# TensorE runs six products into an unread PSUM bank ahead of each look-up of maxima in the attention layer

## What is computed

```python
z = h @ W.T
s_src = z @ w1
s_dst = z @ w2
e = leaky_relu(s_src[src] + s_dst[dst], negative_slope=0.01)
m = segment_max(e, dst, num_segments=n)
num = exp(e - m[dst])
den = segment_sum(num, dst, num_segments=n)
alpha = num / den[dst]
w_e = (rel_alpha * alpha)[:, None]
h_agg = segment_sum(w_e * z[src], dst, num_segments=n)
return h_agg + bias_w
```

## Time and profile before

| | |
|---|---|
| time, median of 3 runs | 9725.82 us (9722.43 to 9730.15) |
| time of the profiled execution | 9727.96 us |
| its span from the first to the last instruction | 9726.4 us |
| attention stage, by the trace | 3338 to 5345 us |
| looks in it | 244 (196 groups, 48 of them with two blocks) |
| granted TensorE clock, mean over the span | 0.872 |

### The profile page before, as it was taken

One profiled execution on the slowest core, in us unless ns is written; L12 is line 12 of the kernel. 1 busy time (PEld: TensorE's weight loads), 2 busy tenths in 40 slices (PEclk: granted clock), 3 DMA queues, 4 the chain that ended last, 5 costly groups with the idle time before them and its releaser, 6 DMA issues. The chain is left out here.

```text
span 9726.4 us, 155325 instructions
## 1 busy us (share of the span) xinstructions
PE 7678.1 (79%) x38400; PEld 4799.3 (49%) x38401; DVE 4294.4 (44%) x10706; ACT 3170.9 (33%) x5260; POOL 5560.6 (57%) x5296
## 2 busy tenths in 40 slices
PE   1698888888888566666665799999999888888886
PEld 0354444444444355555554344444444656666654
DVE  6887777774443466666666210000000323323323
ACT  0012334565555466655554000000000232333232
POOL 4788888887775000000000577777775477777775
PEclk6899999999999766656666899999999999999998
DMA  3223445566666433333222899999999322222222
GB/s 111 73 89 119 143 163 171 201 219 228 212 219 210 148 131 114 112 101 98 94 87 73 292 333 337 345 334 340 324 356 332 117 78 77 77 78 77 77 78 66
DMA packets 563180, 1661.59 MB, mean 171 GB/s; under 512 B 115314, under 2 KB 312030, under 8 KB 519495
## 3 DMA queue, kind: packets, MB, share of 16 engines
q1 hardware_dynamic: 324442, 1129.76, 33.2%
q0 software_dynamic: 206976, 473.99, 16.1%
q10 hardware_dynamic: 31536, 54.94, 1.6%
HBM read 1174.46 MB, written 483.82 MB: 170 GB/s over the span
## 5 line engine op out<-in xcount | busy, mean ns | idle before, releaser
L909 PE MATMUL wide<-ring 128*128 128x392 bf16 x14112 | 2499.8, 339 | 501.7 <-DVE ring L839 262.6
L529 POOL DMA_INDIRECT z_got<-z_table,z_idx x1568 | 2131.9, 1360 | 596.8 <-issue 429.2
L909 PEld LDWEIGHTS wide<-ring 128*128 128x128 bf16 x14112 | 1408.0, 100 | 1593.3 <-issue 821.8
L1578 POOL DMA_INDIRECT l_rows<-h_table,l_recs x1568 | 1564.3, 998 | 626.9 <-issue 477.8
L1487 POOL DMA_INDIRECT sorted_recs<-dn_rec_in,type_f x1568 | 1526.6, 974 | 647.7 <-issue 471.7
L1029 POOL DMA_DIRECT2D rows<-z_edges x196 | 103.9, 530 | 2086.5 <-PE wide L362 1876.8
L1390 PE MATMUL wide<-stream,X 128*128 128x512 f32 (+1 forms) x2548 | 1044.8, 570 | 63.1 <-DMA stream<-c_dense 59.0
L373 PE MATMUL wide<-rows,onehot 128*128 128x130 f32 x3904 | 888.1, 417 | 232.2 <-DVE A L390 232.2
L373 PEld LDWEIGHTS wide<-rows,onehot 128*128 128x128 f32 x3904 | 820.9, 319 | 293.0 <-DVE A L390 291.3
L373 PE MATMUL wide<-l_rows,l_onehot 128*128 128x128 f32 x3904 | 584.0, 311 | 361.9 <-DVE X L391 361.8
L1677 DVE TENSOR_TENSOR l_rows<-l_filters,l_rows 128x1024 f32<-128x1024 f32 x196 | 240.3, 1226 | 1334.3 <-DMA l_rows<-h_table,l_recs 1316.6
(11 more groups left out here) (255 smaller groups left out, 8427.8 us busy)
## 6 DMA issues: line engine op xcount, KB each, us to landing
stream<-w_dense SPq DMA_DIRECT2D x252, 1792.0 KB
stream<-c_dense SPq DMA_DIRECT2D x84, 1792.0 KB
z_edges<-z_got POOLq DMA_DIRECT2D x196, 528.0 KB
rows<-z_edges POOLq DMA_DIRECT2D x196, 528.0 KB, 3.8
dst_bc<-in_dst_row SPq DMA_DIRECT2D x196, 512.0 KB, 3.6
c_dense<-A SPq DMA_DIRECT2D x49, 1568.0 KB
w_dense<-A SPq DMA_DIRECT2D x49, 1568.0 KB
c_dense<-H SPq DMA_DIRECT2D x49, 1568.0 KB
```

The lines of the kernel that those rows point to most:

```text
L529: e.indirect_dma_start(out=z_got[:, s, t, :], out_offset=None, in_=z_table, in_offset=bass.IndirectOffsetOnAxis(ap=z_idx[:, s, t:t + 1], a ...
L909: ins = e.matmul(banks[:, bass.ds(to[v], 1), int(m > 0), 0:WC].rearrange("p a x -> p (a x)"), lhsT=slots[:, k, m * P:(m + 1) * P], rhs=slo ...
L1578: e.indirect_dma_start(out=rows[:, k, t, :], out_offset=None, in_=h_table, in_offset=bass.IndirectOffsetOnAxis(ap=recs[:, k, t, R_DST:R_DS ...
```

## The change

In the loop over the blocks of a group, before the waits for `s_ot` and `s_q`, TensorE now issues 6 products of 512 bf16 columns, with the unit matrix as the stationary operand and the unit matrix repeated four times as the moving one. They write bank 6, which nothing reads, and they wait for nothing and signal nothing. They are called "the fill" below. With 244 looks these are 1464 products. No other instruction is removed, added or moved.

```diff
+FILL = 6
...
                         e.matmul(look, lhsT=zero_h[0:1, :], rhs=zero_h[0:1, 0:6 * TILES], start=True, stop=False)
                         with e.Fori(lo, hi):
                             e.reg_add(c, c, 1)
+                            for _ in range(FILL):
+                                e.matmul(bank[6][:, 0:4 * P], lhsT=ident_h[:, :],
+                                         rhs=ident_h[:, :].unsqueeze(1).to_broadcast([P, 4, P]), start=True, stop=True)
                             e.wait_ge(s_ot, c)
                             e.wait_ge(s_q, c)
                             e.sem_inc(note["pe"], 1)
```

## The result

| | before | after |
|---|---|---|
| median, us | 9724.12 (4 runs) | 9786.75 (4 runs) |
| ratio | | 1.0066, 95% interval 1.0054 to 1.0078 |
| first look to last look, from the trace | 1991 us | 2051 us |

The changed kernel is slower by 63 us, 0.66%. The forecast was 9732 us; the time is inside the range, but on the slower side of it, not within 0.2% of before. The products of the looks start between 3340.7 and 5392.0 us of the span after, against 3338.4 and 5329.6 us before: the whole loss is in the stage of attention.

What follows compares the result with a forecast made beforehand. VectorE was taken to set the pace of attention's one-block groups. Lost 79 us and gained 73 us, net +6 us on 9725.8 us, gave 9732 us; range 9692 to 9795 us for 8 in 10.

Steps and rivals of the forecast that it cites:

- What bounds the stage: In attention, VectorE sets the pace of one-block groups; TensorE's speed counts only in two-block groups, with waits of 65.5 and 70.2 us.
- The fill's own time: Ahead of the look, six products take 2.5 us at 1.2 GHz, or 1.3 at 2.4 GHz, 1.4 with hand-over.
- Second looks: Ahead of the 48 second looks TensorE is idle 4.43 us, so the fill is hidden at either clock: cost 0.
- The price of a late look: First looks behind sums at 1.2 GHz come 1.0 us late, 2.3 if the fill is slow too; the stage grows in full.
- The gain for one pair of blocks: In two-block groups, first-block sums at 2.4 GHz save 1.7 us each, 82 us over all 48.
- How often the clock is up: In attention, 65 of 196 groups are cold at their sums; 43 of 48 two-block sums run fast.
- The sum of +6 us: Whole kernel: 79 us lost to late looks against 73 us gained in two-block groups, net +6 us.
- the slower rival: Clock falls in the 3.42 us between look and sums in 120 groups: net +92 us, 9818 us; chance 0.30.
- the wash: Whole kernel within 19 us of no change, 9707 to 9745 us; chance 0.46.
- The faster one: Attention's clock stays up, falling only behind the 48 second looks: net -34 us, 9692 us; chance 0.22.
- the one with no effect on the clock: Attention's clock stays at 0.62 and every first look is late: +390 us, 10118 us; chance 0.02.
- The page's rule: Clock falls in waits between matmul bursts, so the stretch between look and sums costs at nearly every group: +92 us.

Runs made afterwards that it cites:

- six, two and four: The changed kernel (six products ahead of each look) plus two while TensorE waits for ScalarE and four ahead of the sums; stage 1978 us, ratio to before 0.9979.
- two and four, full rows: Kernel before, plus two products while TensorE waits for ScalarE, four ahead of the sums, and spreading widened to 128 rows; stage 1927 us, ratio 0.9931.

## Why the prediction was right or wrong

- **What bounds the stage.** Right. Behind fast sums nothing got faster in a group of one block, and the gain is only in groups of two.
- **The fill's own time.** Right: 1.46 us for six at 2.4 GHz in the timeline, where 1.3 and a hand-over were forecast.
- **Second looks.** Right: none is late.
- **The price of a late look.** Right: 104.7 us over 103 looks is 1.02 us, forecast 1.0 and a few at 2.3; single looks are 0.1 to 2.1 us late. The delay did add to the stage in full.
- **The gain for one pair of blocks.** Right: 5.18 to 3.58 us is 1.6, forecast 1.7.
- **How often the clock is up.** This is the step that failed, and the prediction had called it open. It took 65 groups as cold at their sums: the 48 behind a second look, and 17 more. The clock was down at the start of the sums behind 95 of 195 last looks, those 48 and 47 more, and in 31 groups of one block it was still up there but fell during the sums. So 103 looks were late and not 65. It took 43 of the 48 first blocks of a pair as fast; 23 ran wholly at 2.4 GHz, 13 in part and 12 not at all, and the two waits that were to fall to some 60 us came to 93.7. So the loss was 104 us and not 79, the gain 42 us and not 73. Both errors have one cause, that the clock falls behind the look more often than in a third of the groups, and they add up to 56 us, about the distance from the forecast to the result. The windows show it, and two experiments confirm it, one by filling the light stretch (73 us back) and one by filling the rows of the products that it already has (56 us back).
- **What was overlooked in that step.** The spreading was counted as 1.7 us of products in the light stretch together with the look. The trace gives their busy time, not how much of the array they use. Made full, beside the fill, they let the clock fall ahead of the sums in 37 of 169 cases and not in 69.
- **The range.** The time is inside it, but the outcome that was given the best chance, within 19 us of before, did not come. The sum of +6 us was a small difference of two terms that were both wrong; the range held because it reached to most of the slower rival.
- **The rivals.** The result lies between the wash and the slower rival, by the slower one's mechanism: 103 late looks, where it was said to decide from about 85 cold groups on. The faster one and the one with no effect on the clock fell. The page's rule (the Trainium skill, "TensorE: Matmul & The Clock Gate", "HAM oscillation — how this bites in real kernels") stood nearer to the result than the sum did: +92 us was taken by it, +6 by the sum, and +63 was measured. It speaks of waits between bursts of matmuls, though, and the trace agrees with it only in part: the stretch that cost the clock in the windows from 3941 to 3944 holds light work, TensorE being busy 0.48, 0.38 and 0.16 of each microsecond.

## What to carry to other kernels

In this kernel a fill that was to keep TensorE's clock up paid only in the stretch in which the clock is lost, not in the gap that was easiest to reach. So read in 1 us windows where the clock rises and where it falls, and fill ahead of the fall. Look at the slack of that place at the lower clock, since the fill takes twice as long (0.43 against 0.22 us a product) just where the clock was lost. Before products are added, see how many rows the existing ones use: widening them with zeros gained 56 us of the stage beside the fill and 20 us beside the one in the light stretch, but nothing without a fill, where the stage was 5 us longer.

## What was not expected of the hardware

- Six products with 32 rows left the granted clock at 0.58 where six with 128 rows, of the same count and columns, and as long at the same clock, brought it to 0.82. Eight spreading products made full changed it from 0.82 to 0.88 beside a fill and from 0.62 to 0.64 without one.
- Without a fill the full rows did not hold the clock: it was up at the end of 104 of 195 last looks and at the start of 19 of the sums behind them.
- Three products ahead of each look cost as much as six: 2052 and 2051 us for the stage.
- A clock of 0.93 in the stage (six, two and four) gave 1978 us and a clock of 0.83 (two and four, full rows) 1927 us: the mean clock of a stage says little of its time; where it is up decides.
